# Moving the routing front, the row batches and the last loads of a two-FFN transformer block

## The reference

```python
x = x + 0.5 * _L0_ffn_ref(_layernorm(x), ...)
x = x + _L0_attn_ref(_layernorm(x), ...)      # 16 heads of width 8, causal
x = x + 0.5 * _L0_ffn_ref(_layernorm(x), ...)

# _L0_ffn_ref: one shared expert for all tokens, two of seven routed experts for each
shared_out = _expert(x, sg, su, sd)            # silu(x @ g.T) * (x @ u.T) @ d.T, hidden 352
probs = jax.nn.softmax(x @ wr.T + rb, axis=-1)
scores, idx = jax.lax.top_k(probs, 2)
scores = scores / scores.sum(axis=-1, keepdims=True)
out = shared_out + sum_e w[..., e] * _expert(x, rg[e], ru[e], rd[e])
```

## Time and profile before

| what | us |
|---|---|
| median of three runs | 620.84 |
| the three runs | 620.44, 620.84, 624.7 |
| the profiled execution, its own time | 620.84 |
| its span, first to last instruction | 618.9 |
| PE busy in the span | 562.3 |
| DVE busy | 456.6 |
| POOL busy | 255.0 |

### The profile page before, as it was taken

The page is one execution under the profiler, slowest core; times in us unless marked ns, Lnnn a source line. Parts: engine busy times, 40 slices in busy tenths (PEclk is TensorE's granted clock), DMA queues, the critical chain, the costliest instruction groups (busy, mean ns, idle before and its releaser), DMA issues.

```text
span 618.9 us, 11864 instructions
## 1 busy us (share of the span) xinstructions
PE 562.3 (91%) x3738; PEld 428.4 (69%) x3738; DVE 456.6 (74%) x1151; ACT 328.7 (53%) x701; POOL 255.0 (41%) x400
## 2 busy tenths in 40 slices
PE   2979999998895889999999999999999999899995
PEld 1859899997773545555555555555564889899895
DVE  3677777778559887877777787877555788577865
ACT  4444444456534435656566665657667434344543
POOL 7387846455243321212111111111235888854440
PEclk9998999999987879999999999999999999899998
DMA  9913236932571453313122221311000122431414
GB/s 258 289 45 84 73 81 155 233 109 76 155 235 51 153 114 94 127 34 110 53 93 69 83 79 63 100 37 58 3 2 14 36 68 60 108 89 34 129 31 111
DMA packets 46888, 58.74 MB, mean 95 GB/s; under 512 B 6183, under 2 KB 37678, under 8 KB 46062
## 3 DMA queue, kind: packets, MB, share of 16 engines
q1 hardware_dynamic: 38160, 46.77, 27.0%
q0 software_dynamic: 4480, 9.25, 4.7%
q10 hardware_dynamic: 4190, 1.98, 1.3%
HBM read 38.09 MB, written 28.00 MB: 107 GB/s over the span
## 4 chain that ended last, share of the span: by engine, by line
PE 69%; DVE 14%; DMA 4%; issue 4%; POOL 4%; ACT 3%; SPq 1%; DVEq 0%; ACTq 0%; POOLq 0%
PE psum L1571 11%; PE psum L1614 10%; PE psum L1636 10%; PE psum L848 5%; PE psum L850 4%; PE psum L849 4%; PE psum L866 4%; PE psum L884 4%; DVE mxp L1718 3%; PE psum L887 3%; POOL z_rows L1108 2%; PE psum L1574 2%; DMA queries<-m_rows 2%; PE psum L907 1%; DVE at_l L1007 1%
## 5 line engine op out<-in xcount | busy, mean ns | idle before, releaser
L1718 DVE TENSOR_REDUCE mxp<-psum 128x1 f32<-128x512 f32 (+3 forms) x304 | 182.7, 656 | 33.8 <-PE psum L1571 28.3
L1775 ACT ACTIVATE probs<-psum 128x512 f32<-128x512 f32 (+1 forms) x304 | 154.8, 580 | 97.9 <-PE psum L1614 79.6
L1571 PE MATMUL psum<-keys,queries 128*128 128x512 f32 (+1 forms) x304 | 118.4, 451 | 4.4 <-DVE mxp L1718 3.7
L1614 PE MATMUL psum<-queries,keys 128*128 128x512 f32 (+3 forms) x384 | 105.2, 366 | 8.0 <-DMA queries<-m_rows 7.4
L1826 POOL TENSOR_SCALAR_AFFINE_SELECT probs<-probs 128x512 f32<-128x512 f32 x64 | 40.6, 635 | 173.0 <-ACT probs L1775 173.0
L1131 POOL DMA_INDIRECT y_rows<-ys,to_row x76 | 74.1, 975 | 88.1 <-DVE ys L1045 56.6
L956 ACT ACTIVATE silu<-psum 128x352 f32<-128x352 f32 x107 | 49.7, 465 | 103.5 <-PE psum L850 103.5
L1001 DVE TENSOR_TENSOR act<-silu,psum 128x352 f32<-128x352 f32 x107 | 55.5, 519 | 46.7 <-ACT silu L956 46.0
L1614 PEld LDWEIGHTS psum<-queries,keys 128*128 128x128 f32 x384 | 65.6, 189 | 32.5 <-ACT probs L1775 16.4
L1571 PEld LDWEIGHTS psum<-keys,queries 128*128 128x128 f32 x304 | 57.5, 198 | 41.8 <-DVE mxp L1718 36.0
L1636 PE MATMUL psum<-probs,vg 128*32 128x512 f32 (+3 forms) x768 | 76.0, 494 | 0.3
(11 more groups left out here) (260 smaller groups left out, 1020.1 us busy)
## 6 DMA issues: line engine op xcount, KB each, us to landing
z_rows<-q_stack SPq DMA_DIRECT2D x12, 682.5 KB, 5.6
keys<-q_stack SPq DMA_DIRECT2D x12, 512.0 KB
keys<-k_stack SPq DMA_DIRECT2D x32, 128.0 KB, 6.4
queries<-q_stack SPq DMA_DIRECT2D x8, 512.0 KB, 6.1
zg_early<-z_rows SPq DMA_DIRECT2D x44, 65.0 KB, 1.9
yc<-y_rows SPq DMA_DIRECT2D x10, 256.0 KB, 3.9
zg_late<-z_rows SPq DMA_DIRECT2D x32, 65.0 KB
k_stack<-zt_h SPq DMA_DIRECT2D x8, 256.0 KB, 3.0
```

The lines of the kernel that those rows point to most:

```text
L1571: ins = e.matmul(dst, K.queries[u][:, i * P:(i + 1) * P], K.keys[u][:, heads[0]:heads[-1] + 1, k0 * P:(k0 + nb) * P], start=True, stop=Tru ...
L1614: ins = e.matmul(slot(K, u, d, n)[:, m * (q1 - q0):(m + 1) * (q1 - q0)], K.keys[v][:, j, kt * P:(kt + 1) * P], K.queries[v][:, q0:q1], sta ...
L1718: e.tensor_reduce(K.mxp[:, heads[0]:heads[-1] + 1, i, which], scores, AX.X, ALU.max).then_inc(K.A["taken"], 1)
L1775: e.activation(K.probs[:, kt % 2, heads[0]:heads[-1] + 1, q0:q1], src, ACT.Exp, scale=SCALE).then_inc(K.A["ex"], 1)
```

## The change

It touches seven things:

1. `BATCHES`: tiles 10 to 13 form one batch of four in place of two batches of two, in both FFNs.
2. In the second FFN the normalised rows of chunk 3 are written by ACT in place of DVE; its `norm_rstd_pool` thereby has four instructions in place of two.
3. The routing of half 1 is spread over steps 3 to 7: "norm_tr" of chunk 2 behind the up projection of step 3 and of chunk 3 behind that of step 4 (both stood ahead of step 4), "logits" of chunk 3 at step 5 (was 4), both parts of "router" behind step 5 (were between and behind step 4), "places" on PE ahead of step 7 (was between, in step 6) and on DVE behind step 6 (was between, in step 6).
4. The first two sorts of the second FFN leave their places among the masks of the last attention group and stand behind all masks, each with a pause, which they did not have.
5. Of half 0's sorts, five in place of eight stand ahead of the two `norm_rstd_pool` calls.
6. ACT issues the last two loads of results behind its last copy, not at step 52.
7. DVE mixes chunk 2 behind its last eviction, not at step 54.

```diff
-BATCHES = [(0, 2), (2, 4), (6, 4), (10, 2), (12, 2)] + [(j, 4) for j in range(14, NJ, 4)]
+BATCHES = [(0, 2)] + [(j, 4) for j in range(2, NJ, 4)]
...
-    return k < 2 or c == 2
+    return k < 2 or c >= 2
...
-    if c == 3:
-        e.wait_ge(K.NS[k]["z"], c)
...
-        for what, c in BETWEEN_DVE[f].get(step, ()):
-            late_dve(K, f, what, c)
...
-    if f == 0 or g % TT > 0:
-        pause_pool(K, f == 1 and t < HALF)
+    pause_pool(K, f == 1 and t < HALF)
...
-        if kind == LAST and kt in (4, 5):
-            sort_part_pool(K, 1, 0, kt - 4, kt - 3)
...
-              {2: (("z", 2),), 3: (("norm_hi", 2), ("norm_hi", 3)), 20: (("tanh", 0),), 38: (("weigh", 0),), 40: (("weigh", 1),), 52: (("results", 1),)}]
+              {2: (("z", 2),), 3: (("z", 3),), 4: (("norm_hi", 3),), 20: (("tanh", 0),), 38: (("weigh", 0),), 40: (("weigh", 1),)}]
...
-               38: (("mix", 0),), 40: (("mix", 1),), 54: (("mix", 2),)}]
+               38: (("mix", 0),), 40: (("mix", 1),)}]
...
-TAIL_PE = {2: (("proj", 2), ("proj", 3)), 4: (("norm_tr", 2), ("norm_tr", 3))}
-BETWEEN_PE = [{}, {1: (("proj_tr", 2), ("proj_tr", 3)), 4: (("logits", 2), ("logits", 3)), 6: (("places", 1),)}]
-BETWEEN_DVE = [{}, {4: (("router", (1, 0)),), 6: (("places", 1),)}]
+TAIL_PE = {2: (("proj", 2), ("proj", 3)), 7: (("places", 1),)}
+BETWEEN_PE = [{}, {1: (("proj_tr", 2), ("proj_tr", 3)), 3: (("norm_tr", 2),), 4: (("logits", 2), ("norm_tr", 3)), 5: (("logits", 3),)}]
...
             ffn_act(K, 1)
+            results_load(K, e, 1, 1, (1,))
...
-            sort_part_pool(K, 1, 0, 2, 4)
+            sort_part_pool(K, 1, 0, 0, 3)
             pad_pool(K, 1)
-            sort_part_pool(K, 1, 0, 4, 8)
+            sort_part_pool(K, 1, 0, 3, 5)
             norm_rstd_pool(K, 2, 2)
             norm_rstd_pool(K, 2, 3)
             ids_pool(K, 1, 1)
-            sort_part_pool(K, 1, 0, 8)
+            sort_part_pool(K, 1, 0, 5)
```

More of the change, by code:

```diff
@@ L2035 @@
             50: (("q", 1),), 51: (("v", 0),), 52: (("v", 1),)}
-BETWEEN_ACT = [{46: (("q1", 0),), 48: (("q", 0), ("q1", 1)), 50: (("q", 1),)}, {}]
+BETWEEN_ACT = [{46: (("q1", 0),), 48: (("q", 0), ("q1", 1)), 50: (("q", 1),)}, {3: (("norm_hi", 2),)}]
 BEHIND_ACT = [{20: (("tanh", 0),), 40: (("weigh", 0),), 42: (("weigh", 1),), 43: (("n_z", 0),), 44: (("n_hi", 0),), 45: (("n_z", 1),),
               46: (("n_hi", 1),), 51: (("v", 0),), 52: (("v", 1),)},
-              {2: (("z", 2),), 3: (("norm_hi", 2), ("norm_hi", 3)), 20: (("tanh", 0),), 38: (("weigh", 0),), 40: (("weigh", 1),), 52: (("results", 1),)}]
+              {2: (("z", 2),), 3: (("z", 3),), 4: (("norm_hi", 3),), 20: (("tanh", 0),), 38: (("weigh", 0),), 40: (("weigh", 1),)}]
 FRONT_DVE = {0: (("router", (1, 0)), ("router", (1, 1))), 2: (("segments", 0), ("lists", (0, 0)), ("lists", (0, 1)), ("lists", (0, 2)), ("lists", (0, 3))), 4: (("places", 1),),
@@ L2043 @@
               46: (("q1_lo", 0), ("n_lo", 1)), 48: (("q_lo", 0), ("q1_lo", 1)), 50: (("q_lo", 1),)},
-              {0: (("proj_lo", 2), ("proj_lo", 3)), 1: (("x", 2), ("stats", 2), ("x", 3), ("stats", 3)), 2: (("z", 3),),
-               3: (("norm_lo", 2), ("norm_lo", 3)), 4: (("router", (1, 1)),), 8: (("segments", 1),), 9: (("lists", (1, 0)),),
+              {0: (("proj_lo", 2), ("proj_lo", 3)), 1: (("x", 2), ("stats", 2), ("x", 3), ("stats", 3)), 3: (("norm_lo", 2),), 4: (("norm_lo", 3),),
+               5: (("router", (1, 0)), ("router", (1, 1))), 6: (("places", 1),), 8: (("segments", 1),), 9: (("lists", (1, 0)),),
                10: (("lists", (1, 1)),), 11: (("lists", (1, 2)),), 12: (("lists", (1, 3)),), 22: (("weights", 0),),
-               38: (("mix", 0),), 40: (("mix", 1),), 54: (("mix", 2),)}]
+               38: (("mix", 0),), 40: (("mix", 1),)}]
 FRONT_POOL = {26: 0, 28: 1}
-TAIL_PE = {2: (("proj", 2), ("proj", 3)), 4: (("norm_tr", 2), ("norm_tr", 3))}
-BETWEEN_PE = [{}, {1: (("proj_tr", 2), ("proj_tr", 3)), 4: (("logits", 2), ("logits", 3)), 6: (("places", 1),)}]
-BETWEEN_DVE = [{}, {4: (("router", (1, 0)),), 6: (("places", 1),)}]
+TAIL_PE = {2: (("proj", 2), ("proj", 3)), 7: (("places", 1),)}
+BETWEEN_PE = [{}, {1: (("proj_tr", 2), ("proj_tr", 3)), 3: (("norm_tr", 2),), 4: (("logits", 2), ("norm_tr", 3)), 5: (("logits", 3),)}]
 TAIL_ACT = {0: (("gather", 2), ("gather", 3), ("proj", 2), ("proj", 3))}
@@ L2087, in late_act @@
         weights_tanh_act(K, f)
-    elif step == "results":
-        results_load(K, K.nc.scalar, f, c, (1,))
     elif step == "silu":
@@ L2267, in _ @@
             ffn_dve(K, 1)
+            mix_dve(K, 1, 2)
             mix_dve(K, 1, 3)
```

## The result

The changed kernel takes 628.32 us (median of 8 runs, 626.1 to 629.49) against 620.51 us (median of 8 runs) for the kernel before on the same chip: ratio 1.0112, 95% interval 1.0081 to 1.0143. Its profiled execution took 629.03 us with a span of 627.2 us, 8.3 more than the 618.9 of before.

A forecast was written before the change was run, and what follows sets the result against it. It took POOL's sorts ahead of tile 10's batch, and the issue of the last loads, to bound the end. Terms 4.2 + 1.0 + 0.2 + 2.0 = +7.4 us on 620.84 gave 628.2 us, range 626.0 to 630.5.

The forecast's parts named there:

- POOL's queue: Ahead of half 1's first sort: longer norm calls, then eleven sorts in place of eight; +4.2 us, bounds 4.0 to 4.4.
- The slots: Ahead of half 1's sorts: ready at 506.1, margin 0.6 us, uncharged; rival, later slots decide: 629.7 us, chance 0.2.
- The wait at tile 0: At the batch of tile 0, PE arrives at about 508.9 and waits 2.1 us, covered by POOL's delay.
- The batch of four: At step 19, PE waits for four loads, not two, 0.51 apart: +1.0 us, bounds 0.5 to 1.2.
- The transposes at the low clock: At tile 10's batch, two more transposes cost 0.48 us and two at step 21 (0.24) go: +0.2 us.
- The tail: At the end, ACT's last loads go later and land in 3.3 us; last sum +2.0 us, bounds 1.5 to 3.4.
- the attention's end: Rival at the last masks: without two sorts among them the attention ends 2.4 us sooner, 625.8 us; chance 0.06.
- The clock staying up at step 19: Rival at tile 10's wait: PE's clock may not fall there, saving 1.5 us, 626.7 us; chance 0.1.
- PE's slack: At tile 10's batch: moving POOL's queue sooner counts only beyond PE's 2.46 us wait; any move later moves the end.

The follow-up runs named there:

- batch_only: The kernel before with item 1 alone (tiles 10 to 13 in one batch of four): ratio 1.0017 (0.9989 to 1.0046).
- pool_order_back: The changed kernel with POOL's order of sorts as before (two among the masks, eight ahead of the norm calls): ratio 1.0105 against the kernel before.
- route_only: The kernel before with items 2 and 3 alone (chunk 3's rows on ACT, routing of half 1 spread): ratio 1.0034.
- tail_only: The kernel before with items 6 and 7 alone (last two loads and chunk 2's mix moved behind): ratio 1.0023 (0.9999 to 1.0046).
- routing_back: The changed kernel with items 2 and 3 undone (routing of half 1 as before): ratio 1.011 against the kernel before.
- no_pause_half1: The kernel before without the pauses behind half 1's sorts, but for the first: 615.92 us, ratio 0.9935.
- the four parts alone: Four kernels, each the kernel before with some items alone: 4 and 5 (1.0044), 2 and 3 (1.0034), 1 (1.0017), 6 and 7 (1.0023).

## Why the prediction was right, point by point

**The sum held**: +7.4 predicted, +8.3 in the span, +7.8 between the medians. No term had the wrong sign, and the two largest were right in mechanism and nearly in size. But each of the four measured stretches lies outside the bounds that I gave its term (4.48 over 4.4, 1.24 over 1.2, 1.26 over 0.5, 1.34 under 1.5), and the two large misses, +1.1 and -0.7, partly cancel: how close the sum came is in part luck.

- **POOL's queue.** Right in each step. The calls began at 486.07 (485.85 predicted) with POOL idle 1.32, the next sort at 490.34 (490.29), half 1's first at 507.72 (507.48), its last at 531.21 (530.9). +4.48 for +4.2: the period of the sorts was taken as 1.563 throughout, but the first one behind the calls takes 1.10, not 0.97, and the next follows 1.71 later (492.05), in the kernel before too (489.83 to 491.55).
- **The slots.** Ready at 506.01, predicted 506.1, with a margin of 507.72 - 0.81 - 506.01 = 0.9 in place of 0.6. Relative to the last mask they moved by 3.6 (29.43 against 25.85), which is the 1.35 + 2.25 of the working. That rival was close, since a low clock in the routing as in batch_only could have used the margin up: pool_order_back and route_only show that without POOL's own delay the slots decide.
- **The wait at tile 0.** Wrong in its form. PE was to come at 508.9 and wait 2.1; it came at 511.14 without a wait, having run at 1.2 GHz from 505 to 511. The claim that this is covered by POOL was right: tile 10 still made PE wait 2.10. All three profiles with the spread routing have that fall and no wait; with the old routing and POOL's delay the wait is there, and is 3.22.
- **The batch of four.** +1.24 for +1.0, a hair over the upper bound of 1.2. Four loads took 1.84 from first to last, not 3 x 0.51 = 1.53, against 0.51 for two: +1.33. The landing was 0.1 shorter.
- **The transposes at the low clock.** +0.2 predicted, +1.26 found in the stretch (the 0.5 that the sum took as its high bound stands nowhere in the working). The term itself held: from the batch of tile 10 to that of tile 14 it is 10.01 for 9.83, +0.18. But the working behind it didn't: the batch of four took only 0.65, since the clock fell just behind it, so the doubled price of two transposes isn't where the 0.18 comes from. What the sum left out is 1.1 us between the batches of tiles 18 and 22:

```profile
556.20 0.63 PE L905 MATMUL psum<-ident,zg_early 128*128 128x128 f32 x4
565.84 0.63 PE L905 MATMUL psum<-ident,zg_late 128*128 128x128 f32 x4
```

These 9.64 us are 8.50 in the kernel before (550.35 to 558.85), and the clock is at 1.00 in both. They lie where this silu on ACT began though its up projection (the last matmul of L848 at 557.47) had been done for 1.2 us:

```profile
558.97 0.47 ACT L954 ACTIVATE silu<-psum 128x352 f32<-128x352 f32 x1 [0.93 <-PE psum L848]
```

No other experiment with the changed routing or batches shows this loss (their stretches are 73.66 to 74.99), so it may belong to this execution; its cause is open. A loss of 1.0 us, again with a late silu, stands between the batches of tiles 2 and 6 (10.08 us from start to start, 9.07 before), where PE's wait at tile 10 covers it.
- **The tail.** +1.34 for +2.0, mis-sized. The loads went 3.26 later than SP's (3.4 predicted). The first landed 2.9 us behind its issue and the second 3.4, before ACT had weighed the first, so that ACT weighed both in one go of 2.45. I had taken 3.3 for the first. The low end of my bounds, 2.9, was the right row, though it gave 1.5 and not 1.34. tail_only repeats it.
- **The rivals.** No move of the attention's end shows beyond its scatter of 3.6 us (the masks shown waited for ACT). The clock staying up at step 19 didn't come in this profile. It did in pool_order_back and routing_back, which lack one part each, with 1.3 to 1.7 us less than before in the stretch behind, the rival's 1.5; and in routing_back just as it was told, with a wait and a fall at step 9 first. So the median may hold executions of both kinds: the eight runs have granted clocks of 0.961 to 0.973, and the fastest has the highest, but no second profile of this kernel was taken.
- **PE's slack, told the wrong way round.** The first paragraph says that sorts that end sooner move the end only beyond PE's 2.46 us. PE waits for them, so the first 2.46 are what counts, and more brings nothing: in no_pause_half1 the last sort came 4.2 us sooner behind the last mask, and the stretch to tile 10 is 2.6 shorter. The sum has only shifts the other way and doesn't use it.

**The parts don't add as the sum suggests.** The ratios of the four parts alone sum to 0.44 + 0.34 + 0.17 + 0.23 = 1.18%, near the 1.12% of the whole. That is chance: POOL and routing alone make 3.7 and 3.4 us of delay at half 1's first sort and 4.5 together, while each alone gets 1.1 to 1.4 us back behind tile 10.

## What to carry to other kernels

Where an instruction waits for two things that are ready at nearly one time, price the later of the two after the change, and expect that undoing either cause gives little back. When a transfer is moved behind work, count its issue time in full, but take the landing from rows with as few transfers in flight as it will have. A pause in a queue of indirect DMAs that looks like waste should be taken out only with several variants of the kernel timed: here one variant won 0.65% and four close relatives, one of them with the same work, lost 2.2 to 3.5%.

## What the runs showed of the hardware

- POOL's indirect DMAs of 128 rows of 130 floats take 0.96 us each and follow each other at 1.264 us without a pause, 1.563 with a memset of 384 elements between.
- With sorts at 1.264 us, PE, DVE and ACT stood nearly still together for 10 to 15 us in four kernels of five, for a reason that the profile doesn't show; with sorts at 1.563, in none of nine.
- PE's granted clock fell behind a wait of 2.10 us and held behind one of 2.23, in executions of different kernels. A fall cost 1.3 to 1.5 us of work in three executions and 2.6 in a fourth, and in the one profile with ten idle matmuls in the wait it didn't come.
